# A two-layer graph attention kernel: first-layer wh products moved into steps 5 to 7, second-layer ones a step later, and fourteen matmuls put at the head

## The reference

```
for l in range(2):
    Wh, Ws = split(x @ W[l], 2, axis=-1)
    scores = Wh @ Ws.T                       # 4096 x 4096
    a = softmax(scores, axis=-1) * adj
    x = leaky_relu(a @ Wh + x, 0.01)
out = layernorm(x0 + x)                      # x0: the input
```

## Time and profile before

| | |
|---|---|
| three timed runs | 1590.10, 1594.44, 1595.33 us, median 1594.44 |
| profiled execution | 1591.92 us; span 1590.1 us |
| mean granted TensorE clock | 0.998 |
| PE busy | 1552.6 us (98% of the span) |
| DVE busy | 1345.5 us (85%) |
| ACT busy | 645.4 us (41%) |
| POOL busy | 802.9 us (50%) |
| DMA | mean 190 GB/s |

### The profile page before, as it was taken

The page is one execution under the profiler, slowest core; times in us unless marked ns, Lnnn a source line. Parts: engine busy times, 40 slices in busy tenths (PEclk is TensorE's granted clock), DMA queues, the critical chain, the costliest instruction groups (busy, mean ns, idle before and its releaser), DMA issues. The chain is left out here.

```text
span 1590.1 us, 23354 instructions
## 1 busy us (share of the span) xinstructions
PE 1552.6 (98%) x8104; PEld 1315.7 (83%) x8104; DVE 1345.5 (85%) x1577; ACT 645.4 (41%) x1177; POOL 802.9 (50%) x799
## 2 busy tenths in 40 slices
PE   8999999999999999999799999999999999999996
PEld 7888888888888888888687888888888888888885
DVE  5778877887887788788847899999999999999998
ACT  5344344444444344444433444443444444334432
POOL 0155555555555555555412555555555555555555
PEclk9999999999999999999999999999999999999999
DMA  5377777776777777777924777777777877787775
GB/s 166 116 190 202 184 201 191 193 200 190 193 193 198 187 198 195 195 199 209 256 79 127 197 192 213 191 200 190 205 203 197 207 198 203 186 208 193 202 217 147
DMA packets 166981, 302.57 MB, mean 190 GB/s; under 512 B 39760, under 2 KB 67408, under 8 KB 166736
## 3 DMA queue, kind: packets, MB, share of 16 engines
q1 hardware_dynamic: 104800, 131.84, 33.0%
q0 software_dynamic: 37200, 135.28, 30.1%
q10 hardware_dynamic: 24864, 33.98, 8.0%
HBM read 157.29 MB, written 9.44 MB: 105 GB/s over the span
## 5 line engine op out<-in xcount | busy, mean ns | idle before, releaser
L1223 POOL TENSOR_TENSOR a_lo<-turned,a_hi 128x512 fp32r<-128x512 f32 x488 | 629.8, 1305 | 623.8 <-ACT a_hi L831 621.9
L659 PE MATMUL banks<-wh,a_hi 128*128 128x512 f32 x1952 | 699.9, 398 | 13.8 <-POOL a_lo L1223 13.8
L799 ACT ACTIVATE ring<-banks,neg_max 128x1024 f32<-128x1024 f32 x256 | 286.1, 1117 | 862.0 <-DVE neg_max L979 848.2
L661 PE MATMUL banks<-wh,a_lo 128*128 128x256 f32 x1952 | 548.1, 281 | 0.0
L659 PEld LDWEIGHTS banks<-wh,a_hi 128*128 128x128 f32 x1952 | 367.4, 188 | 105.3 <-POOL a_lo L1223 11.8
L979 DVE TENSOR_REDUCE neg_max<-banks 128x1 f32<-128x1024 f32 x256 | 312.0, 1219 | 156.6 <-PE banks L544 156.5
L542 PE MATMUL banks<-x_t,q_t 128*128 128x512 f32 x1024 | 406.9, 397 | 2.5 <-DVE q_t L943 1.8
L544 PE MATMUL banks<-x_t,q_t 128*128 128x512 f32 x1024 | 402.4, 393 | 0.0
L543 PE MATMUL banks<-x_t,q_t 128*128 128x512 f32 x1024 | 400.3, 391 | 0.0
L661 PEld LDWEIGHTS banks<-wh,a_lo 128*128 128x128 f32 x1952 | 368.9, 189 | 7.9
L1019 DVE SCALAR_TENSOR_TENSOR ring<-ring,weight,load 128x1024 f32<-128x1024 f32 x251 | 326.3, 1300 | 0.6 <-DMA load<-adj 0.4
(11 more groups left out here) (97 smaller groups left out, 892.4 us busy)
## 6 DMA issues: line engine op xcount, KB each, us to landing
load<-adj POOLq DMA_DIRECT2D x254, 512.0 KB, 5.2
turned<-ring SPq DMA_DIRECT2D x1500, 64.0 KB, 4.1
turned<-ring ACTq DMA_DIRECT2D x500, 64.0 KB, 3.3
rows<-x SPq DMA_DIRECT2D x32, 128.0 KB, 3.3
x_scratch<-rows SPq DMA_DIRECT2D x32, 128.0 KB, 3.1
rows<-x_scratch SPq DMA_DIRECT2D x30, 128.0 KB, 3.6
first_rows<-x SPq DMA_DIRECT2D x30, 128.0 KB, 3.1
out<-rows SPq DMA_DIRECT2D x30, 128.0 KB, 3.2
```

Source lines behind the costliest of these rows:

```text
L659: nc.tensor.matmul(psum[:, bank, :], of_hi[:, b], wh[:, k].rearrange("p a d -> p (a d)"), start=start, stop=stop, skip_group_check=True)
L661: last = nc.tensor.matmul(psum[:, bank, 0:D], of_lo[:, b], wh[:, k, 0], start=False, stop=stop, skip_group_check=True)
L799: nc.scalar.activation(ring_at(i).rearrange("p (r b j) -> p b r j", r=2, j=QUAD), psum[:, 2 * (i % 2):2 * (i % 2) + 2, :].rearrange("p h ( ...
L1223: nc.gpsimd.tensor_tensor(operand(1, j).rearrange("p b (r j) -> p b r j", r=QUADS), as_f32(turned_in[unit_place(unit)][:, :, b:b + SUB, :] ...
```

## The change

The number of wh sides behind each step's scores, first layer: before, two behind each of steps 0 to 7; now two behind step 0, two behind step 5, six behind step 6 and six behind step 7. Second layer (its last eight sides): before, two behind each of steps 4 to 7; now two behind step 5, three behind step 6 and three behind step 7. The second layer's weight work is done one step later in each of its two parts (steps 2 and 3 instead of 1 and 2). All wh sides of the first layer from the third on are wide (before, only the ninth and later ones). Fourteen transposes of the unit matrix, which nobody reads, are put ahead of `transpose_w(0)`, into bank 7.

```
-            return {0: [("x", 6), ("x", 7)], 1: [("wt", 1)], 2: [("w", 1)]}.get(step, [])
+            return {0: [("x", 6), ("x", 7)], 2: [("wt", 1)], 3: [("w", 1)]}.get(step, [])
...
-        WH_AFTER = [{n: 2 for n in range(8)}, {n: 2 for n in range(4, 8)}]
+        WH_AFTER = [{0: 2, 5: 2, 6: 6, 7: 6}, {5: 2, 6: 3, 7: 3}]
...
-            wide = kind == "wh" and n % WPAIRS >= EARLY
+            wide = kind == "wh" and (n >= WPAIRS + EARLY or WH_AFTER[0][0] <= n < WPAIRS)
...
             pe.wait_ge(ident_done, 1)
+
+            for _ in range(14):
+                nc.tensor.transpose(psum[:, ACC_BANK + 1, 0:P], ident[:], ident[:])
             transpose_w(0)
```

## The result

The changed kernel took 1597.12 us (median of 15 runs, 1593.96 to 1599.4) where the kernel before took 1593.36 us (median of 15, 1590.1 to 1595.33). The ratio is 1.0023, 95% interval 1.0016 to 1.003: some 3.7 us slower. That is less than the 0.3% that the prediction asks of a change, but the interval leaves out 1, so the slowdown is small and not noise. The profiled execution took 1597.99 us with a span of 1596.1 us, against 1591.92 and 1590.1 us before.

The account below looks back on a forecast made before the run. PE was taken to bound the kernel, issuing without gaps between its waits. Head -0.6, first layer 0 and second layer +1.05 gave +0.45 us, so 1594.9 us from the 1594.44 median; range 1590 to 1598 us.

Parts of the forecast that it names:

- the likeliest case alone: Whole kernel: the range for the forecast case without the other rivals, 1592.5 to 1597 us.
- The head, -0.6: Kernel start: fourteen transposes raise PE's clock at 5.0 to 5.9 us, amid the weight's transposes, saving 0.6 us.
- The first layer's walk, 0: First layer: product waits of 2.29 and 0.52 us go, waits of 1.2 and 1.4 us come; sum 0.
- From that weighing on all is as before: First layer, after chunk 3's weighing at 72.95 us: the chain is unchanged, third product at 81.80 us.
- The second layer, +1.05: Second layer: earlier weighing gives -0.67 us, but a 3.05 us q-side wait loses the clock, costing 1.7 us.
- both branches of the forecast: Second layer: +1.05 us if the clock falls behind the q side's wait, -0.67 us if it holds.
- A: The forecast itself: clock lost behind the second layer's q-side wait, 1594.9 us; chance 0.42.
- B: Second layer: the clock holds as in the first, -1.3 us in all, 1593.2 us; chance 0.34.
- C: Second layer: clock falls at the q side's wait and stays low until the products, +7.2 us, 1601.6 us; chance 0.06.
- D: Both layers: the predicted waits are absent and the earlier ones vanish, -9 us, 1585.4 us; chance 0.10.
- E: Head: the added matmuls do not lift the clock and save nothing, 1595.5 us; chance 0.08.
- The rule on transposes: Head: transposes don't count as clock work like matmuls, so the head would save nothing; given a small chance.

Follow-up runs that it names:

- e2: The kernel before with only the fourteen head matmuls added, no side moved: 1595.68 us, ratio 1.0004 to before.
- e9: e8 with all eight block moves of chunks 1 and 3 of each layer issued by SP: 1589.45 us, ratio 0.9975 to before.
- e11: The changed kernel run once more, unedited: ratio 1.0034 to the kernel before.
- e1: The changed kernel without the fourteen head matmuls, so the moved sides alone: 1596.74 us, ratio 1.0015 to before.
- e3: The changed kernel without head matmuls and with the second layer's sides as before, so the first layer's part alone: 1594.57 us, ratio 1.0000 to before.
- e5: The changed kernel with eight head matmuls instead of fourteen: ratio 1.0019 to the kernel before.
- e6: The kernel before with twenty head matmuls added and no side moved: 2.3 per thousand slower than before (ratio interval 1.0014 to 1.0032).
- e8: The changed kernel, head matmuls kept, with step 6's q side made ahead of the wh sides in both layers: 1593.79 us, ratio 0.9995 to before.
- e4: The kernel before with only the second layer's sides moved (2, 3, 3 behind steps 5, 6, 7): 1596.46 us, ratio 1.0004 to before.
- e7: The changed kernel without head matmuls, with step 6's q side made ahead of the wh sides in both layers: 1593.59 us, ratio 0.9993 to before.

## Why the prediction was right or wrong

- **The time** was forecast at 1594.9 us, the same within 0.3%, in a range of 1590 to 1598. 1597.12 lies in the range and the class is right, but the ratio's interval (1.0016 to 1.003) excludes the 1.0003 that the forecast says. It is a loss of 3.8 us where 0.45 was forecast. That the number comes within 2.2 us is in part luck: the forecast started from a median of three runs, 1594.44 us, and the median of fifteen is 1593.36. The range of the likeliest case alone (1592.5 to 1597) is missed by a little.
- **The head, -0.6: wrong in the profiled execution.** Chunk 1's scores start at 25.06 for 25.04 us. The eight transposes of the weight take 1.97 for 1.94 us: fourteen matmuls ahead, busy from 1.57 us on, had not raised the clock by 4.83. It rose at 7.1 us, not at 5.0 to 5.9 (the x transposes behind them took 1.30 us for 1.91), and M stayed at 9.18 with a wait of 1.28 for DVE. In e2, e9 and e11 it did rise at 5.9, 5.4 and 5.1 us and M came at 8.75, 8.49 and 8.37; e11 lost that gain again in x's groups, which then waited 0.41 and 0.23 us for their loads (25.01 us in all), while e2 and e9 kept 0.4 and 0.7 us. What the step missed is the other side of it: without the matmuls the clock rose at 13.2 to 13.9 us in two of the six kernels that have none (e1 and e3), and in e5 with eight, and the head took 2 us more. None of the six with fourteen or twenty did.
- **The first layer's walk, 0: right up to the third product, and there the failed step.** The waits at M (1.12 for 1.2 forecast), at the fifth side (1.24 for 1.4), the scores (71.38 for 71.5) and the first product (74.21 for 74.3) were as forecast. The step that failed is "From that weighing on all is as before", with the third product at 81.80. What broke it is not in PE's order at all: one DMA issue of ACT took 2.36 us instead of 0.87, and behind the moves stand the exponentials of chunk 8 and the high parts of chunk 1, from which POOL makes the low parts that the third product waits for (2.98 us). The prediction took the three moves at their usual length; it had no term for an issue that is held. e1 and e3, with the same sides moved and no stall, took 56.65 and 56.69 us; e6, with no side moved and a stall, took 58.36.
- **The second layer, +1.05: the mechanism right, the size too small.** Wait before the q side and loss of clock were there. e1, which is this step without a stall, lost 0.98 us (+1.05 forecast), and e5, with the same wait of 2.94 us and the clock held, gained 0.57 (0.67 forecast). So without a stall both branches of the forecast come true. The changed kernel lost 2.32: its wait was 4.42 for 3.05 us, because one of ACT's three moves at 847.69 took 2.10 us instead of 0.87. That is some 1.3 us more.
- **What is left of the sum.** The middle and the last stretch are 0.92 and 0.81 us longer in the profiled execution. No side was moved there. In the nine traces without a clock loss at the middle's start (before and after among them) the middle lies between 745.8 and 747.4 us, and in all thirteen the last stretch lies between 714.5 and 717.9, so the two differences are within what executions differ by. The other four are e5, e6, e8 and e11. All had a stall in the first layer, and in all the clock was low for 3.4 us just behind the third product (from 84.9, 83.2, 82.6 and 83.6 us). Their middles are 748.5 to 749.8 us, some 2 us longer. The profiled execution of the changed kernel had the stall and not this loss, so a stall in the first layer can cost 2 us more than the +1.90 of the table. The prediction has no such term.
- **The rivals.** A (clock lost behind the q wait) was what happened in the profile, e1, e4 and e11; B (it holds, 1593.2) in e5, with the same wait of 2.94 us as e1 and e4. The length of the wait does not decide it: in the first layer the changed kernel kept the clock behind 2.98 us, and e5 lost it behind 1.86. What does is not shown. C (the clock stays low) has its nearest case in e4, with 6.8 us low and +2.1 us, not the +8.5 of matmuls at half speed that 1601.6 was made of. By its own price, half of a low stretch is lost, so a loss that makes up +4.8 us needs some 12 us low and not the 7 that it says. D (the waits vanish) is refuted by the rows at 55.32 and 853.84. E (head gives nothing) was true of the profiled execution and of e11, added to A.
- **The rule on transposes.** The prediction weighed the Trainium skill, "TensorE: Matmul & The Clock Gate", section "Part 4: PE-mode transpose", by which transposes on TensorE don't bring its clock up. The runs contradict it for these fp32 transposes of 128x128: in e2, e9, e11 and e6 the clock rose at 4.7 to 5.9 us, when PE had done nothing but transposes since 1.57 us. e6's head shows it. Twenty take 3.91 us where the changed kernel's first fourteen alone take 3.25, and the eight of the weight 1.04, for 1.94 in the earlier trace rows:

```profile
1.57 3.91 PE L668 MATMUL banks<-ident 128*128 128x128 f32 x20 [1.57 <-POOL ident L1220]
5.32 1.04 PE L552 MATMUL banks<-ident,ring 128*128 128x128 f32 x8
6.19 1.05 PE L585 MATMUL banks<-ident,ring 128*128 128x128 f32 x8
8.72 0.39 PE L542 MATMUL banks<-turned 128*128 128x256 f32 x1 [1.49 <-DVE turned L946]
```

The last row also says why so little comes of it. The transposes of x end at 7.24 us, 1.25 us earlier than in the earlier trace rows (8.49), but M starts only 0.44 us earlier, since it waits 1.49 us for DVE.
- **A rule that was not weighed and should have been.** The Trainium skill, "Runtime: NRT & Kernel Launch", section "Instruction fetch mechanics", has the sequencer read its instructions in blocks of 16 KiB, 256 instructions, by a DMA queue of its own, and calls the crossing of a block mostly hidden. The first half agrees with the trace: 63 packets for 16,208 instructions, one per 257. For PE no row here speaks against the second. But the DMA issues of ACT and SP that meet a packet take up to 2.36 and 2.87 us, and of that the section says nothing.

**What stays open.** That stall and packet fall together is shown (e5 and e6 placed it by the count of PE's instructions, and e1 and e7 moved it away). By what resource one holds the other is not: no view shows where the issue waits. Nor is it shown why 230 of the 650 packets that overlap an issue hold none for over 1.2 us. What share of the measured +3.7 us is the stall is known only from profiled executions: +1.9 and some +1.3 us in one, and in e11 1.3 to 1.4 us a layer over e1, with the clock loss behind the first. Whole times don't confirm a share: e1 without a stall in its trace is at 1.0015, and e8 with one is no slower than e7 without. And each kernel of the experiments has one trace, so how often a stall, a late clock in the head or a loss of clock comes in a kernel's other runs is open.

## What to carry to other kernels

When the path runs through an engine that also issues DMAs between its computing, price its queue as part of the path, and give the issues to an engine with slack: here the exponentials waited for three moves that cost 2.07 us, and at times 4.02. A count of instructions on the busiest engine is no neutral change: 28 matmuls and weight loads that nobody reads moved a packet onto another engine's issue, and in the changed kernel's trace that cost more than the head could give. Before crediting or blaming moved work, compare stretches between instructions that both kernels have, against a kernel that shifts the instructions without moving the work.

## What the runs showed of the hardware

- DMA issues on ACT that take 0.87 us elsewhere took 2.36, 2.10, 2.22 and 1.99 us where an instruction packet of PE (16 KB) overlapped them, and one of 0.62 took 1.90. Of all issues over 1.2 us in thirteen traces 96% overlapped such a packet, and most ended some 0.37 us behind it.
- The granted clock of the head rises at different times in executions of nearly the same work: 4.7 to 8.4 us in ten of thirteen, 13.2 to 13.9 in three. The late rise costs 2 us.
- A wait of 2.94 us cost the clock in e1 and e4 and did not in e5; one of 2.98 us in the changed kernel did not, and one of 1.86 us in e5 did. Where it was lost, it was at 0.50 for about 3.4 us, in e4 for 6.8.
